# A Fourier layer stack with 3x3 convolutions in one kernel: halo kept once, side columns and corners as 32x32 products

## The chip, the cores and the metric

The kernel runs on one core of a Trainium2 chip. The metric is device time in microseconds (us), the median of several executions. Five engines work beside each other, each through its own instruction stream: PE (TensorE, matmuls), DVE (VectorE), ACT (ScalarE), POOL (GpSimd, which also issues the stores here) and SP (SyncE, which issues the loads). They meet at semaphores.

## The reference, cut to what matters

```python
h = concatenate([grid, x]) @ P_w + P_b                  # 32 images of 64x64, 32 channels
for i in range(4):
    h_ft = rfft2(h)
    out_modes = einsum('bixy,ioxy->boxy', h_ft[:, :, :16, :16], w_c)   # w_c complex
    spec = irfft2(out_modes, s=(64, 64))
    conv = conv_general_dilated(h, conv_w[i], (1, 1), 'SAME') + conv_b[i]   # 3x3
    h = leaky(spec + conv)
out = leaky(h @ Q1_w + Q1_b) @ Q2_w + Q2_b              # the "head", one value a pixel
h = out + attention(layernorm(out)); h = h + experts(layernorm(h))          # the tail
```

All of it is in fp32.

## The kernel before

Images go in pairs: 16 pairs a layer, 4 layers; `T = 16 * layer + pair` counts them. A pixel's parity in y and x (the "phase") stands on the partitions beside the 32 channels: 4 phases x 32 channels = 128 partitions, and a pair has 2 x 32 rows of 32 columns, cut in four units of 16 rows, one PSUM bank each (`acc[0]` to `acc[3]`, 512 columns).

One pair in the two middle layers (1 and 2, function `pair`) does this on PE. `convolve_centre` (L648): four products of 128x128 by 512 columns, one a unit, all taps that stay inside the 2x2 phase cell. `spectral` (L694): 64 products of 64x64 by 64 columns, the last step of the inverse transform, into the same four banks. `convolve_rows` (L662), twice: the taps that reach the phase cell above or below, and the corner taps. `rows_forward` (L553): the first transform of the pair's successor. `convolve_columns` (L676), twice: the taps to the left and right. `columns_back` (L620) and `columns_forward` (L566): two more transform steps of the next pair.

A product whose operands cover 64 partitions in and 32 out takes one of 8 places in the array, and 8 such products can run together; I call eight that fill the array (or one 128x128 product) a round of 512 columns. `convolve_rows` is 2 rounds a call, `convolve_columns` 1, so the edge work of a pair is 6 rounds in 48 products. The head's first product (`head_hidden`, L712) is of 32x32 by 512 columns. There are 16 a pair, in two groups of 8, since `hidden` has two banks.

The input of the convolution is `halo`, one pair's activations with a border, in SBUF in two copies: one with the phases ordered for rows, one for columns. They come from DRAM (`activations`), where POOL put them (`store`, four DMAs a pair) when the layer before made them: ACT evicts the four banks (`evict`, L1092) to `x_now`, DVE turns `x_now` (`turn_x`, L1283) into `xt` for `rows_forward`, `turn_rows` (L1289) and `turn_back` (L1312) turn the transform's other steps, ACT puts the spectrum away (`spectrum`, L346). SP loads the halo (`load_halo`, L406 and L412) when the pair two before has been accumulated.

Layer 0 convolves otherwise (L633), since its input is small. Between layers stands `boundary`: it needs the whole spectrum before `mix` (L605). In the last layer (`last_pair`) there is no forward transform; there PE also does the head of the pair before and steps of the tail, `fronts` (L735 to L769), put in by the table `SLOTS` at places 0, 1 and 2 of a pair. The order on each engine is the order of the code; waits are written out by hand.

Of the kernel before, what the change touches and what calls it, by code (L numbers as in the profile page):

```python
# [14 lines left out]
C = 32  # L15
NL = 4
MODES = 16
G = 32
# [4 lines left out]
HALO = TOP + PLANE + 2 * PITCH + 1  # L23
# [8 lines left out]
XCOL = 48  # L32

# [7 lines left out]
def dft_constants():  # L41
# [8 lines left out]
    for at in range(2):  # L50
        a = th * np.outer(2 * g + (at ^ (g >= 16)), k)
        ex[:, at, :, 0] = np.cos(a)
        ex[:, at, :, 1] = -np.sin(a)
# [8 lines left out]
    for qh in range(2):  # L62
        for kbh in range(2):
            for cg in range(2):
                for ql in range(2):
                    k1 = 4 * (2 * kbh + cg) + 2 * qh + ql
                    for il in range(2):
                        for at in range(2):
                            a = th * k1 * (4 * i16 + 2 * il + (at ^ (i16 >= 8)))
# [19 lines left out]
def build(nc, ser_d, xcol_d, fixed_d, dft_d, fold_w_d, fold_p_d, proj_d, spec_d, conv_d, convb_d,  # L89
# [4 lines left out]
    with ExitStack() as ctx:  # L94
# [16 lines left out]
        conv = sb("conv", [128, NL - 1, 512])  # L111
        centre = [conv[:, l, 0:256].rearrange("p (a n) -> p a n", a=2) for l in range(NL - 1)]
        edge_y = [conv[:, l, 256:320].rearrange("p (a n) -> p a n", a=2) for l in range(NL - 1)]
        edge_x = [conv[:, l, 320:448].rearrange("p (v a n) -> p v a n", v=2, a=2) for l in range(NL - 1)]
        corner = [conv[:, l, 448:512].rearrange("p (a n) -> p a n", a=2) for l in range(NL - 1)]
# [7 lines left out]
        halo = sb("halo", [128, 2, 2, HALO])  # L123
# [13 lines left out]
        hidden = psum[:, 4:6, :]  # L137
# [25 lines left out]
        s_side = [sem("s_side0"), sem("s_side1")]  # L163
# [64 lines left out]
        spare_h = flat(halo, "p k a n -> p (k a n)")  # L228
        squares = spare_h[:, 0:1024].rearrange("p (k n) -> p k n", k=2)
        spread = spare_h[:, 1024:2048].rearrange("p (k n) -> p k n", k=2)  # L230
        late = spare_h[:, 2048:8192].rearrange("p (a k n) -> p a k n", a=6, k=2)
        alive = spare_h[:, 2048:4096].rearrange("p (b s) -> p b s", b=B)
        fx, live, hx, hm, ht, fo = (late[:, n] for n in range(6))
# [96 lines left out]
        def units(T):  # L330

            return (0, 1, 2, 3) if T < PAIRS else (0, 2, 1, 3)

        def evicted(T, u):

            return 4 * T + units(T).index(u) + 1
# [36 lines left out]
        def halo_loads(T):  # L373

            return 128 * ((T - PAIRS) // 2 + 1)
# [3 lines left out]
        def _(sp):  # L379
# [15 lines left out]
            def load_halo(T):  # L395
                l, p = place(T)
                k, src = T % 2, T - PAIRS
                sp.wait_ge(s_store[src % 2], 64 * (src // 2 + 1))
                if src >= 2:
                    sp.wait_ge(s_acc, 4 * (T - 2) + 4)  # L400
                n = 2 * UNIT
                for h in range(2):
                    to, of = TOP + n * h, n * h
                    for f in range(4):
                        g = 32 * (2 * (f % 2) + (f // 2 ^ h))
                        sp.dma_start(halo[32 * f:32 * f + 32, k, 0, to:to + n],  # L406
                                     x_d[p, g:g + 32, of:of + n]).then_inc(s_halo[k], 16)
                for h in range(2):
# [1350 lines left out]
```

## Time and profile before

| | |
|---|---|
| median of 3 runs | 1119.27 us (1118.8 to 1122.3) |
| profiled execution, its own time | 1122.64 us |
| its span | 1120.5 us |
| PE busy | 1049.3 us (94%) |
| DVE, ACT, POOL busy | 604.0, 464.3, 152.9 us |
| granted PE clock, mean | 0.985 |
| moved by DMA | 194.27 MB |

The span is what the trace covers; the execution's own time has about 2 us more around it. Busy shares are means over four layers and a tail of different kinds. "issue" in a row is time in which an engine waited for nothing that the profile shows. A product in fp32 stands in the trace as two weight loads and two matmuls, so `x64` in a row of L662 is 32 products.

### The profile page before, as it was taken

The numbers are of one execution on the slowest core, as the hardware profiler recorded it, in microseconds if no ns is written. First come the engines' busy times: TensorE is split into PE (matmuls) and PEld (weight loads), VectorE is DVE, ScalarE is ACT, GpSimd is POOL, SyncE is SP. The second block draws the span as 40 slices with busy tenths as digits, with TensorE's granted clock in tenths as the row PEclk, the third lists the DMA queues.
The fourth block names the chain that finished last, engine by engine and source line by source line (L and its number), as shares of the span: only waits on it lengthen the run. The fifth ranks groups of instructions, "written<-read, shape, count | busy, mean of one in ns | idle before, by whom it ended". The sixth has DMA issues, their size and how long they took to land.

```text
span 1120.5 us, 48730 instructions
## 1 busy us (share of the span) xinstructions
PE 1049.3 (94%) x22512; PEld 556.8 (50%) x22512; DVE 604.0 (54%) x560; ACT 464.3 (41%) x895; POOL 152.9 (14%) x299
## 2 busy tenths in 40 slices
PE   5899998899999999899999998999999999899985
PEld 2555554555555554654555555434444334366743
DVE  5688788655556665555556565201322303387844
ACT  3356553323333333133343342232443534666524
POOL 2022221011111111011111110102112121300000
PEclk9999998999999999999999999999999999899998
DMA  9277768279888888488988886578766453000001
GB/s 321 60 221 214 200 176 249 84 216 270 252 260 258 254 232 238 137 245 254 258 257 267 234 237 192 148 163 197 188 144 147 120 125 82 8 2 1 1 1 19
DMA packets 66714, 194.27 MB, mean 173 GB/s; under 512 B 22256, under 2 KB 24816, under 8 KB 59248
## 3 DMA queue, kind: packets, MB, share of 16 engines
q1 hardware_dynamic: 54224, 138.19, 45.4%
q0 software_dynamic: 12288, 52.97, 16.5%
q8 instruction: 177, 2.90, 1.1%
q14 instruction: 25, 0.20, 0.1%
HBM read 138.13 MB, written 52.95 MB: 171 GB/s over the span
## 4 chain that ended last, share of the span: by engine, by line
PE 84%; DVE 7%; issue 5%; ACT 3%; DMA 0%; DVEq 0%; ACTq 0%
PE psum L662 16%; PE psum L648 15%; PE psum L694 11%; PE psum L676 7%; PE psum L620 5%; PE psum L566 4%; PE psum L553 4%; PE psum L633 4%; PE psum L712 3%; PE psum L605 2%; PE psum L903 2%; PE psum L720 1%; DVE xt L1283 1%; DVE ft L1289 1%; DVE vt L1312 1%
## 5 line engine op out<-in xcount | busy, mean ns | idle before, releaser
L1092 ACT ACTIVATE x_now<-psum,conv_bias 128x512 f32<-128x512 f32 x256 | 155.2, 691 | 321.6 <-PE psum L676 248.4
L1312 DVE STREAM_TRANSPOSE vt<-psum 128x1024 f32<-128x1024 f32 x64 | 126.2, 1972 | 198.8 <-PE psum L620 198.8
L1283 DVE STREAM_TRANSPOSE xt<-x_now 128x1024 f32<-128x1024 f32 x100 | 199.4, 2032 | 15.1 <-ACT x_now L1092 8.9
L1289 DVE STREAM_TRANSPOSE ft<-psum 128x1024 f32<-128x1024 f32 x50 | 100.5, 2010 | 188.4 <-PE psum L553 188.4
L662 PE MATMUL psum<-halo,conv 64*32 64x512 f32 x3072 | 189.0, 593 | 3.5 <-issue 3.4
L346 ACT ACTIVATE spec<-psum 32x128 f32<-32x128 f32 x372 | 143.7, 386 | 92.3 <-PE psum L566 88.5
L648 PE MATMUL psum<-halo,conv 128*128 128x512 f32 x384 | 178.0, 605 | 0.7 <-ACT x_now L1092 0.7
L497 POOL DMA_DIRECT2D activations<-x_now x192 | 94.3, 492 | 600.4 <-PE psum L662 408.5
L694 PEld LDWEIGHTS psum<-dft,vt 64*64 64x64 f32 x8192 | 126.5, 135 | 50.0 <-issue 49.8
L694 PE MATMUL psum<-dft,vt 64*64 64x64 f32 x8192 | 135.8, 220 | 2.2 <-issue 2.2
L648 PEld LDWEIGHTS psum<-halo,conv 128*128 128x128 f32 x384 | 68.5, 188 | 83.5 <-issue 74.7
L662 PEld LDWEIGHTS psum<-halo,conv 64*32 64x32 f32 x3072 | 55.1, 106 | 107.0 <-issue 104.8
L676 PE MATMUL psum<-halo,conv 64*32 64x512 f32 x1536 | 97.0, 591 | 0.0
L620 PE MATMUL psum<-zt,dft 64*32 64x256 f32 x2048 | 77.5, 377 | 10.1 <-issue 7.1
L553 PE MATMUL psum<-xt,dft 64*32 64x512 f32 x800 | 62.1, 602 | 13.5 <-DVE xt L1283 11.1
L620 PEld LDWEIGHTS psum<-zt,dft 64*32 64x32 f32 x2048 | 46.4, 106 | 52.3 <-issue 41.8
L1099 ACT ACTIVATE xt<-psum,q1b 128x512 f32<-128x512 f32 x64 | 40.5, 683 | 68.5 <-PE psum L712 68.3
L566 PEld LDWEIGHTS psum<-dft,ft 128*32 128x32 f32 x3200 | 48.5, 111 | 37.6 <-DVE ft L1289 28.9
L633 PE MATMUL psum<-xcol,conv 96*128 96x512 f32 x128 | 64.7, 632 | 0.4 <-ACT x_now L1092 0.4
L566 PE MATMUL psum<-dft,ft 128*32 128x64 f32 x3200 | 57.5, 223 | 7.2 <-DVE ft L1289 4.5
L504 POOL DMA_DIRECT2D tower_out<-ft x64 | 31.8, 504 | 206.1 <-ACT ft L1106 190.0
L676 PEld LDWEIGHTS psum<-halo,conv 64*32 64x32 f32 x1536 | 31.0, 106 | 50.6 <-issue 45.5
(158 smaller groups left out, 800.5 us busy)
## 6 DMA issues: line engine op xcount, KB each, us to landing
halo<-activations SPq DMA_DIRECT2D x768, 132.0 KB, 3.4
activations<-x_now POOLq DMA_DIRECT2D x192, 264.0 KB, 4.3
wspec<-in_spec SPq DMA_DIRECT2D x64, 256.0 KB, 5.4
xcol<-in_xcol SPq DMA_DIRECT2D x16, 384.0 KB, 5.4
x_now<-in_ser SPq DMA_DIRECT2D x2, 1024.0 KB, 6.5
spec<-in_onehot SPq DMA_DIRECT2D x8, 256.0 KB, 5.7
wspec<-in_causal SPq DMA_DIRECT2D x8, 256.0 KB, 6.2
consts<-in_tail SPq DMA_DIRECT2D x6, 185.0 KB, 5.7
```

What stands on the lines that cost most here:

```text
L346: return copy(spec[g:g + 32, 64 * qh:64 * qh + 64, ql, 2 * p:2 * p + 2].rearrange("p (y x) b -> p y b x", x=MODES), columned(X + 2)[32 * q ...
L566: z = mm(columned(n)[g:g + 32, 64 * kyb:64 * kyb + 64], ft[:, k0, :], ey[:, ri, :], start=(ri == 0), stop=(ri == 1))
L620: z = mm(backed[g:g + 32, cg, 256 * ri:256 * ri + 256], iy[64 * cg:64 * cg + 64, m, 32 * h:32 * h + 32], zt[64 * cg:64 * cg + 64, :, 2 * p ...
L633: mm(acc[u], conv0[:, u // 2, :], xcol[0:96, k, HALF * u:HALF * u + HALF], start=True, stop=False, skip_group_check=True)
L648: mm(acc[u], centre[l - 1][:, u // 2, :], window(T, 0, None, u, 0, 0), start=True, stop=False, skip_group_check=True)
L662: z = mm(acc[u][g:g + 32, :], weight[64 * f:64 * f + 64, s, :], window(T, 0, f, u, di, dj), start=False, stop=False, skip_group_check=True)
L676: z = mm(acc[u][g:g + 32, :], edge_x[l - 1][64 * f:64 * f + 64, h, r, :], window(T, 1, f, u, 0, -1 if s == 0 else 1), start=False, stop=p > 0,
L694: z = mm(acc[u][64 * s:64 * s + 64, at:at + 64], vt[64 * il:64 * il + 64, k, 4 * u + ih].rearrange("p r o -> p (r o)"), ix[64 * il:64 * il ...
L1092: copy(x_now[:, k, 16 * u:16 * u + 16, 0:G], acc[u].rearrange("p (i j) -> p i j", j=G), ACT.Prelu, bias=conv_bias[:, l:l + 1], alpha=SLOPE ...
L1283: vec.transpose(xt[:, 32 * m:32 * m + 32, :], src).then_inc(s_xt, 1)
L1289: vec.transpose(ft[:].rearrange("p k c -> p c k"), rowed.rearrange("p a b -> p (a b)").rearrange("p (i c) -> p c i", c=C)).then_inc(s_ft, 1)
L1312: vec.transpose(vt[:, k].rearrange("p h r o -> p (h r) o").rearrange("p y o -> p o y"), backed.rearrange("p a b -> p (a b)").rearrange("p ...
```

## The change

The halo is kept once (rows order only), with three things for it.

- Phases of a unit are stored in another permutation, one that depends on the unit's half and parity (`u // 2`, `u % 2`). `load_halo` becomes one DMA of 128 partitions and four of 32 (was 16 of 32). `store` becomes eight DMAs (was four), each with half the rows, and they wait for other points of PE's work.
- The edge work of a pair is 5 rounds in 64 products: `convolve_rows`, 2 calls of 8 products of 64x32, one round each, without the corners; `convolve_sides`, 3 calls of 16 products of 32x32, for corners (tap 0), and side columns (taps 1 and 2). Tap 2 runs ahead of `rows_forward`, taps 0 and 1 at the pair's end, after `columns_back`. All four banks are complete only with tap 1.
- `hidden` has four banks (4 to 7) and `head_hidden` is one group of 16 products. The `fronts` of places 0 and 1 come behind it, each behind a wait for ACT to have read two of these banks.

```diff
-                n = 2 * UNIT
-                for h in range(2):
...
-                        sp.dma_start(halo[32 * f:32 * f + 32, k, 0, to:to + n],
-                                     x_d[p, g:g + 32, of:of + n]).then_inc(s_halo[k], 16)
...
+                sp.dma_start(halo[:, k, TOP:TOP + REACH], x_d[p, :, 0:REACH]).then_inc(s_halo[k], 16)
+                for f in range(4):
+                    g = 32 * (f ^ 1)
+                    sp.dma_start(halo[32 * f:32 * f + 32, k, TOP + REACH:TOP + 2 * REACH],
+                                 x_d[p, g:g + 32, PLANE - REACH:PLANE]).then_inc(s_halo[k], 16)
...
-                    elif i == 2:
-                        pool.wait_ge(s_fx, P + 2)
-                    elif i == 3:
-                        pool.wait_ge(s_acc, 4 * P + 2)
                     else:
-                        pool.wait_ge(s_seg, 2 * (P - PAIRS) + 1 + i)
...
+                    elif i < 2:
+                        pool.wait_ge(s_half, 2 * P + 1 + i)
+                    else:
+                        pool.wait_ge((s_fx, s_v)[i - 2], P + 2)
+                    rows = x_now[32 * i:32 * i + 32, X % 2].rearrange("p (h w i) j -> p w h (i j)", h=2, w=2)
+                    for w in range(2):
+                        g = 32 * (2 * (i % 2 ^ w) + i // 2)
+                        pool.dma_start(x_d[X % PAIRS, g:g + 32].rearrange("p (h w n) -> p w h n", h=2, w=2)[:, w],
+                                       rows[:, w]).then_inc(s_store[X % 2], 16)
...
+            def convolve_rows(T, h):
+                for s in range(2):
+                    for f in range(2):
+                        for w in range(2):
+                            r, u = 1 - f, 2 * h + w
+                            g, part = 32 * (2 * s + (r ^ w)), slice(64 * f, 64 * f + 64)
+                            mm(acc[u][g:g + 32, :], edge_y[l - 1][part, h, s, :],
+                               window(T, part, u, (-1 if r == 0 else 1), 0), start=False, stop=False,
...
+            def convolve_sides(T, tap):
+                if tap == 0:
+                    pe.wait_ge(s_seg, T - PAIRS + 1)
+                for u in range(4):
+                    h, w = u // 2, u % 2
+                    for a in range(2):
+                        for b in range(2):
+                            r, s = (a if tap == 2 else 1 - a), 1 - b
+                            g, f = 32 * (2 * s + (r ^ w)), 32 * (2 * a + (b ^ h))
+                            part = slice(f, f + 32)
+                            z = mm(acc[u][g:g + 32, :], sides[l - 1][part, tap, h, :],
+                                   window(T, part, u, 0 if tap > 0 else -1 if r == 0 else 1, -1 if s == 0 else 1),
+                                   start=False, stop=(tap == 1 and p > 0), skip_group_check=True)
+                    if tap == 1 and p > 0:
+                        z.then_inc(s_acc, 1)
+                if tap == 2:
+                    z.then_inc(s_seg, 1)
...
+            def head_hidden(p):
+                pe.wait_ge(s_x, 4 * ((NL - 1) * PAIRS + p) + 4)
+                reached(pe, s_h, p)
+                for u in range(4):
                     for g in range(4):
-                        to = 32 * (g ^ (u % 2))
+                        to = 32 * (g ^ u)
...
             def last_pair(p):
...
+                    convolve_sides(T, 2)
+                    fronts_read(p - 1, 2)
+                    head_hidden(p - 1)
+                    convolve_rows(T, 0)
+                    pe.wait_ge(s_hid, 4 * (p - 1) + 2)
                     fronts(p, 0)
-                    fronts_read(p - 1, 2)
-                    head_hidden(p - 1, 0)
-                    convolve_rows(T, 0)
                     convolve_rows(T, 1)
+                    pe.wait_ge(s_hid, 4 * (p - 1) + 4)
                     fronts(p, 1)
-                    head_hidden(p - 1, 2)
-                    convolve_columns(T, 0)
-                    convolve_columns(T, 1)
+                    convolve_sides(T, 0)
+                    convolve_sides(T, 1)
```

On PE, one pair of a middle layer before, in products: L648 is the centre, L694 the inverse transform, L662 the rows and corners, L553 the forward rows, L676 the columns, L620 and L566 the other transform steps.

```order
L648 MATMUL psum<-halo,conv 128x512 x4
L694 MATMUL psum<-dft,vt 64x64 x64
L662 MATMUL psum<-halo,conv 32x512 x32
L553 MATMUL psum<-xt,dft 32x512 x8
L676 MATMUL psum<-halo,conv 32x512 x16
L620 MATMUL psum<-zt,dft 32x256 x16
L566 MATMUL psum<-dft,ft 32x64 x32
```

The same pair now; the lines have moved: L637 is the centre, L684 the inverse transform, L664 `convolve_sides`, L543 the forward rows, L648 `convolve_rows`, L610 and L556 the other transform steps.

```order
L637 MATMUL psum<-halo,conv 128x512 x4
L684 MATMUL psum<-dft,vt 64x64 x64
L664 MATMUL psum<-halo,conv 32x512 x16
L543 MATMUL psum<-xt,dft 32x512 x8
L648 MATMUL psum<-halo,conv 32x512 x16
L610 MATMUL psum<-zt,dft 32x256 x16
L664 MATMUL psum<-halo,conv 32x512 x32
L556 MATMUL psum<-dft,ft 32x64 x32
```

`rows_forward` stands behind 16 edge products instead of 32, and the last 32 are of the 32x32 kind, between two other kinds.

On PE, the pair of the last layer that carries steps S (L744) and E (L749) of the tail, before: L712 is the head's first product, L720 its second.

```order
L648 MATMUL psum<-halo,conv 128x512 x4
L694 MATMUL psum<-dft,vt 64x64 x64
L744 MATMUL psum<-proj 64x64 x8
L712 MATMUL psum<-x_now,q1w 32x512 x8
L662 MATMUL psum<-halo,conv 32x512 x32
L749 MATMUL psum<-consts,series 128x128 x4
L712 MATMUL psum<-x_now,q1w 32x512 x8
L676 MATMUL psum<-halo,conv 32x512 x16
L620 MATMUL psum<-zt,dft 32x256 x16
L720 MATMUL psum<-xt,q2w 32x512 x4
```

Now, with L699 the head's first product, L731 and L736 the steps S and E, L707 the head's second product:

```order
L637 MATMUL psum<-halo,conv 128x512 x4
L684 MATMUL psum<-dft,vt 64x64 x64
L664 MATMUL psum<-halo,conv 32x512 x16
L699 MATMUL psum<-x_now,q1w 32x512 x16
L648 MATMUL psum<-halo,conv 32x512 x8
L731 MATMUL psum<-proj 64x64 x8
L648 MATMUL psum<-halo,conv 32x512 x8
L736 MATMUL psum<-consts,series 128x128 x4
L664 MATMUL psum<-halo,conv 32x512 x32
L610 MATMUL psum<-zt,dft 32x256 x16
L707 MATMUL psum<-xt,q2w 32x512 x4
```

Between S and E there stand 8 products now, where there were 40; and S stands behind the head's 16.

On ACT at the same place before: L1099 evicts the head's hidden layer, L1122 is the exponential of step S, L1126 the copy of step E.

```order
L1106 ACTIVATE ft<-psum,q2b 128x512
L1122 ACT_TABLE_LOAD
L1122 ACTIVATE series<-fold_p 64x4x64 x2
L1099 ACTIVATE xt<-psum,q1b 128x512 x2
L1126 ACTIVATE fold_w<-psum 128x512
L1099 ACTIVATE xt<-psum,q1b 128x512 x2
L1092 ACTIVATE x_now<-psum,conv_bias 128x16x32 x4
```

And now, with L1089, L1112 and L1116 in their places:

```order
L1096 ACTIVATE ft<-psum,q2b 128x512
L1089 ACTIVATE xt<-psum,q1b 128x512 x4
L1112 ACT_TABLE_LOAD
L1112 ACTIVATE series<-fold_p 64x4x64 x2
L1116 ACTIVATE fold_w<-psum 128x512
L1082 ACTIVATE x_now<-psum,conv_bias 128x16x32 x4
```

The table load and the exponential now stand behind all four evictions of the hidden layer.

## Rows read from the trace of the kernel before

**Rows 1.** The page: busy time and instructions of each engine.

```profile
PE 1049.3 (94%) x22512; PEld 556.8 (50%) x22512; DVE 604.0 (54%) x560; ACT 464.3 (41%) x895; POOL 152.9 (14%) x299
```

**Rows 2.** Chain of waits, one middle-layer pair: start us, us, what.

```profile
584.79 3.64 PE psum L648 x8
588.43 2.02 PE psum L694 x128
590.45 3.60 PE psum L662 x64
594.05 0.86 PE psum L553 x16
594.91 1.72 PE psum L676 x32
596.63 0.86 PE psum L620 x32
597.49 1.03 PE psum L566 x64
```

**Rows 3.** The same view, one last-layer pair without a tail step.

```profile
762.05 1.02 PE psum L712 x16
763.07 3.60 PE psum L662 x64
...
767.68 1.88 PE psum L676 x32
769.56 0.86 PE psum L620 x31
770.42 0.99 PE psum L720 x8
```

**Rows 4.** Stretches, layers 1 and 3: us, each engine's busy us, clock, DMA share, GB/s.

```profile
231.76:442.33 210.57, 209.88 (x5134) 110.33 (x5129) 122.96 (x66) 80.64 (x175) 29.38 (x60) 1.00 0.88 252
709.43:947.07 237.64, 236.14 (x4418) 96.98 (x4419) 54.38 (x83) 98.58 (x161) 39.47 (x78) 1.00 0.63 152
```

**Rows 5.** Chain of waits: a stall inside L662.

```profile
620.11 0.89 issue
```

**Rows 6.** Timeline of PE, eight starts: start, us from first start to last end.

```profile
898.33 0.66 PE L712 MATMUL psum<-x_now,q1w 32*32 32x512 f32 x8
```

**Rows 7.** Groups by line: busy us, mean ns of one, idle before.

```profile
L712 PE MATMUL psum<-x_now,q1w 32*32 32x512 f32 x512 | 34.8, 600 | 0.9 <-DVE sq L1340 0.9
```

**Rows 8.** Timeline of ACT, then DVE, behind one pair's last round.

```profile
639.07 2.42 ACT L1092 ACTIVATE x_now<-psum,conv_bias 128x512 f32<-128x512 f32 x4 [8.01 <-PE psum L676]
641.83 3.21 ACT L346 ACTIVATE spec<-psum 32x128 f32<-32x128 f32 x8 [0.34 <-PE psum L566]
...
642.79 4.09 DVE L1283 STREAM_TRANSPOSE xt<-x_now 128x1024 f32<-128x1024 f32 x2
```

**Rows 9.** Timeline of ACT, last layer: table load, step S, hidden evictions.

```profile
873.79 1.28 ACT L1122 ACT_TABLE_LOAD   x1
881.09 0.84 ACT L1122 ACTIVATE series<-fold_p 64x256 f32<-64x256 f32 x2 [6.02 <-DVE fold_p L1362]
...
899.53 1.26 ACT L1099 ACTIVATE xt<-psum,q1b 128x512 f32<-128x512 f32 x2 [3.25 <-PE psum L712]
```

**Rows 10.** Chain of waits: step S on PE.

```profile
879.67 0.46 PE psum L744 x16
```

**Rows 11.** Chain of waits at the boundary into layer 3, some of its pieces.

```profile
680.46 2.41 ACT x_now L1092 x4
...
700.97 1.88 PE psum L662 x32
702.85 0.95 PE psum L620 x32
...
708.71 0.68 ACT x_now L1092
```

**Rows 12.** The page, DMA issues: KB each, median us to landing.

```profile
activations<-x_now POOLq DMA_DIRECT2D x192, 264.0 KB, 4.3
```

More of the change, by code:

```diff
@@ L110, in build @@
         conv_bias = sb("conv_bias", [128, NL])
[L111 to L115, printed above, removed]
+        conv = sb("conv", [128, NL - 1, TAPS])
+        centre = [conv[:, l, 0:512].rearrange("p (h w n) -> p h w n", h=2, w=2) for l in range(NL - 1)]
+        edge_y = [conv[:, l, 512:640].rearrange("p (h s n) -> p h s n", h=2, s=2) for l in range(NL - 1)]
+        sides = [conv[:, l, 640:832].rearrange("p (t h n) -> p t h n", t=3, h=2) for l in range(NL - 1)]
         fold_w = sb("fold_w", [128, 4, 128])
@@ L136, in build @@
         backed = psum[:, 6:8, :]
-        hidden = psum[:, 4:6, :]
+        hidden = psum[:, 4:8, :]
         valued = psum[:, 4, :]
@@ L810, in pair @@
                     return
-                for u in units(T):
+                for u in range(4):
                     convolve_centre(T, u)
@@ L827, in last_pair @@
                 if p > 0:
-                    for u in units(T):
+                    for u in range(4):
                         convolve_centre(T, u)
@@ L853, in boundary @@
                 T = l * PAIRS
-                for i, u in enumerate(units(T - 1)):
+                for u in range(4):
                     convolve_centre(T, u)
-                    if l == 1 and i == 1:
+                    if l == 1 and u == 1:
                         columns_forward(T)
+                convolve_sides(T, 2)
                 rows_forward(T + 1)
@@ L1647, in phases @@
         q = a.reshape(n, G, 2, G, 2).transpose(4, 2, 0, 1, 3)
[L1648 removed]
+        return np.concatenate([q[:, ::1 - 2 * (u % 2), :, 8 * u:8 * u + 8] for u in range(4)], axis=3)
     ser = np.zeros((2, 2, 2, C, G, 2, PITCH), np.float32)
@@ L1696, in tower_inputs @@
         for b in range(2):
-            for r in range(2):
+            for h in range(2):
                 for s in range(2):
-                    centre[a, b, :, :, 0, s, r] = tap(a - r, b - s)
-                    centre[a, b, :, :, 1, s, 1 - r] = tap(a - r, b - s)
-                edge_x[b, a, :, :, 0, r] = tap(a - r, 1 - 2 * b)
-                edge_x[1 - b, 1 - a, :, :, 1, r] = tap(a - r, 1 - 2 * b)
-            for s in range(2):
-                edge_y[a, b, :, :, s] = tap(1 - 2 * a, b - s)
-                if b != s:
-                    corner[a, b, :, :, s] = tap(1 - 2 * a, 2 * s - 1)
-    conv = np.concatenate([a.reshape(128, NL - 1, -1) for a in (centre, edge_y, edge_x, corner)], axis=2)
+                    for r in range(2):
+                        for w in range(2):
+                            centre[a, b ^ h, :, :, h, w, s, r ^ w] = tap(a - r, b - s)
+                    edge_y[a, b ^ h, :, :, h, s] = tap(1 - 2 * a, b - s)
+                out = 1 - 2 * b
+                sides[a, b ^ h, :, :, 0, h] = tap(1 - 2 * a, out)
+                sides[a, b ^ h, :, :, 1, h] = tap(2 * a - 1, out)
+                sides[a, b ^ h, :, :, 2, h] = tap(0, out)
+    conv = np.concatenate([a.reshape(128, NL - 1, -1) for a in (centre, edge_y, sides)], axis=2)
     fold_p = np.zeros((4, C, 4, 2, 48), np.float32)
```

144 lines of the change are left out of this document (49 added, 95 removed).

## The prediction

> **What bounds the kernel now.** I read the page's busy line first: PE is busy 94% of the span, DVE 54%, ACT 41% [rows 1]. Then the chain of waits through one pair of a middle layer: it stays on PE from end to end, in seven blocks that add up to 13.73 us [rows 2]. So a middle pair costs what PE's blocks cost, and what the others do beside it is hidden as long as none of it ends after PE arrives. The last layer's pair replaces L553 and L566 by two head blocks of 1.02 and the head's second product, 0.99, and its L676 costs 1.88 [rows 3]; with L648 and L694 as in rows 2 it is 15.03 us. The stretches tell what lies above that floor: layer 1 spends 210.57 us on 15 pairs, against 15 x 13.73 = 205.95, so 4.6 us of stalls, at a DMA share of 0.88 [rows 4]. One such stall is 0.89 us of "issue" inside L662 [rows 5].
>
> **The price of a round.** L553 and L676 are one and two rounds of the 64x32 kind behind the same kind: 0.86 and 1.72 [rows 2]. L662 is four, 3.44, and costs 3.60, since it follows L694, which is 64x64. L712, a round of eight 32x32 products, costs 1.02, and L676 behind it 1.88 in place of 1.72 [rows 3]. So a change of kind costs 0.16 us. Eight products start one after another: 0.66 us from the first start to the last end [rows 6], one alone 0.60 [rows 7], so starts are 7 to 8 ns apart. Sixteen reach 0.05 us further, and the next kind waits for the last of them.
>
> **Middle pairs (30, 15 in each of layers 1 and 2).** Removed: one of six edge rounds, -0.86. Added: two changes of kind (32x32 to 64x32 ahead of `rows_forward`, back behind `columns_back`; the others are in the rows already), +0.32, and twice the longer tail of sixteen, +0.10. Net -0.44 a pair, if sixteen 32x32 products fill a round as eight 64x32 do: -13.2 us. That price is the one thing no row of before shows. Its lower end is 0.86, what 512 columns cost in every kind of these rows that fills or half fills the array. Its upper end is that only eight of this kind run at once, as L712's do [rows 3]: 1.72. I take 0.86: issue is not near a limit, since L694 gets through 64 products in 2.02 us, 32 ns each [rows 2], where sixteen in 0.86 need 54 ns.
>
> The Trainium skill speaks against this in TensorEngine Tiling (Array Packing), "Gotcha 1: PSUM Pressure": different row tiles cannot access the same PSUM bank at once. Here the four products of a unit are of four row groups and go to one bank. The trace has this already and does not agree: L712's eight products are four row groups into each of two banks, and they cost 1.02 with the change of kind [rows 3].
>
> In TensorE: Matmul & The Clock Gate, "Part 3: Packing small matmuls — row/col tiling", the Trainium skill has sixteen 32x32 products together at 10.6 times one, and a reorder window of 64 entries on PE. By that page a round of sixteen, each product two loads and two matmuls (L712 has 512 matmuls for 256 products [rows 7]), just fits. No row here shows it.
>
> **Do the waits stay hidden?** All four banks now end together, in tap 1. From the start of L712 at 898.33 [rows 6] to ACT's start behind it at 899.53 [rows 9] there are 1.20 us. So if R is the start of the last round, ACT starts to evict at R+1.16 (the first bank needs four of the sixteen). Four evictions take 2.42, one 0.69 of it [rows 8]: the first bank is free at R+1.85, all at R+3.6. PE does `columns_forward` from R+1.05 to R+2.15, so the centre product does not wait (0.3 to spare). DVE's two turns, 4.09 [rows 8], end at R+7.75. PE comes to `rows_forward` after 1.05 + 1.10 + 3.64 + 2.02 + 1.07: R+8.9, 1.1 to spare. ACT's spectrum, 3.21 [rows 8], ends at R+6.8, and is needed at the same point. All hidden; if the turn came later than that, each tenth would cost 3 us over 30 pairs. POOL's eight store issues lie beside 13 us of PE (POOL is busy 14% [rows 1]). SP issues 5 loads for 16, and the halo bytes fall from 16 x 32 x 4224 B = 2.16 MB to 2 x 128 x 4488 B = 1.15 MB a pair.
>
> **Last layer (15 pairs).** New blocks: 3.64 + 2.02; then one stretch of 32x32 with a sides round and the head round, 1.72 + 0.16 + 0.05 = 1.93; rows, 1.88; two sides rounds, 1.93; then 0.86 and 0.99: 13.25, against 15.03. But PE now waits for ACT. With H the start of the head round, ACT starts at H+1.24 (1.20 and the longer tail). Two evictions take 1.26 [rows 9], the second two end 1.14 later. The wait for two ends at H+2.56, where PE arrives at H+1.93: 0.63 lost. The wait for four ends at H+3.69, where PE arrives at H+3.58: 0.11, and 0.03 of restart. So 14.02, -1.0 a pair. In the three pairs with steps S and E it is less: ACT is at the hidden evictions until H+3.64, then loads its table, 1.28, then does the exponentials, 0.84 [rows 9]; in the old order the load ran in an earlier gap. E can start at H+5.82; S, 0.46 [rows 10] and a change of kind, and a round have taken PE to H+4.15: 1.67 lost, so -0.3 in these three. Sum: 12 x 1.0 + 3 x 0.3 = -12.9 us.
>
> **Boundaries (3).** The rows call behind `mix` is one round instead of two and lies on the chain: 1.88 [rows 11] becomes 1.02, -2.6 in three. The evictions ahead of it, 2.41 [rows 11], start 0.8 later against the end of the rounds than when two banks were ready early: +1.6 for the two boundaries that follow such a pair. The sides rounds lie beside `turn_back`. The store two pairs back now waits for `columns_back`, which ends at 703.80; two issues and 4.3 us to landing [rows 12] end about 709, where the eviction that needs it stands at 708.71 [rows 11]: +0.4 twice. Sum -0.2. The end of the last pair, one head round earlier but waiting for ACT either way: -0.5, from -1 to 0.
>
> **Stalls.** Layer 1 has 4.6 us above its floor [rows 4]. Fewer bytes should shorten such stalls, 64 products for 48 lengthen them: 0, from -6 to +5 in all. Layer 0 keeps its PE work: 0, from -2 to +3 for the doubled store issues.
>
> **The sum.** -13.2 - 12.9 - 0.2 - 0.5 = -26.8. The profiled execution took 1122.6 us by its own time (1120.5 its span), so 1095.8. It stands 3.4 above the median shown, 1119.3, and I forecast on the median: 1092.5.
>
> **Rivals.**
> 1. *Eight at once.* Of the 32x32 kind only eight products run together, and a round of sixteen costs 1.72. There are 48 convolutions with three such rounds, 144, and 16 head rounds: 160 x 0.86 = +138, so 1230. For it: the rows show eight together, never sixteen. Against: the sixteen have sixteen places of their own, and the eight of L712 run at full rate in half of them. From 26.8 / 160 = 0.17 us a round on, the kernel is slower than before.
> 2. *A short window.* All sixteen run together, but behind each change of kind the second eight start 0.28 us late, because PE's queue does not reach so far: two such blocks in 48 convolutions, 96 x 0.28 = +27, so 1119, no change. At a third of that 1101. Nothing in the rows reaches past eight, so nothing speaks against it but that L694's issue is quick.
> 3. *The turn is late.* DVE and ACT end 2 us later than rows 8 give: L553 waits 0.9 in 30 pairs, +27, 1119. Against: four blocks of PE stand between.
> 4. *Stalls grow* by half a us in 45 pairs, since more instructions have to be brought in behind L694: +22, 1115. Against: DMA has less to move.
> 5. *Row groups take turns at a bank.* The four row groups of a unit run one after another, 3.44 a round, +2.58 x 160 = +413, so 1505. Against: L712 [rows 3]. The bank rule of the Trainium skill's page above is this.
>
> **Chances.** The forecast, with its own range 1083 to 1102: 0.66. Rivals 2, 3 or 4 in part (1102 to 1115.9): 0.15. In full, within 0.3% of before (1115.9 to 1122.6, which a measurement cannot tell from no change): 0.05. Slower: rival 1, 0.09; rival 5, 0.01; a stronger rival 2, 0.04. So faster by over 0.3% 0.81, within 0.05, slower 0.14. The range that leaves out two tenths is 1082 to 1113.
>
> **What would show it.** A middle pair at 13.3, with its two sides blocks at 1.07 and 1.93; under rival 1 they are 1.9 and 3.6, under rival 2 the pair is 13.7 to 13.9 and the block behind the inverse transform near 1.3. Rival 3 shows `rows_forward` waiting for DVE. In the last layer: PE waiting for the hidden evictions, 0.6 and 0.1 us a pair, pairs of 14.0, and in three pairs for the exponential. DMA share in layer 1 falls from 0.88 to about 0.7. I am wrong if sixteen 32x32 products behind their own kind cost over 1.0 us.

## The result, and the profile after

The changed kernel takes 1143.05 us (median of 4 runs, 1138.25 to 1144.38) against 1119.03 for the kernel before in the same comparison: recorded ratio 1.0185, 95% interval 1.015 to 1.0219 (the two medians alone give 1.0215). It is slower, by about 2%; the forecast was 1092.5, with a range from 1082 to 1113. The profiled execution took 1141.75 us, its span 1139.6. By stage of the two profiled spans (us); a pair's period runs from its first centre product to the next pair's, the last pair's to the next layer's:

| | before | after | |
|---|---|---|---|
| layer 1, 15 pair periods; shortest | 210.57; 13.73 | 211.23; 13.69 | +0.7 |
| layer 2, 15; shortest | 212.14; 13.73 | 218.38; 13.69 | +6.2 |
| layer 3, 14; shortest | 237.64; 15.03 | 242.99; 14.81 | +5.3 |
| from the last pair's centre products to the end | 173.4 | 179.3 | +5.9 |
| all else, boundaries among it | 286.8 | 287.7 | +0.9 |

The page's lines for PE, for the group of the 32x32 products, and for the queue that brings instructions (packets, MB, share of 16 engines):

```profile
PE 1049.1 (92%) x24048; PEld 554.5 (49%) x24048; DVE 609.0 (53%) x560; ACT 459.4 (40%) x895; POOL 261.6 (23%) x491
L664 PE MATMUL psum<-halo,conv 32*32 32x512 f32 x4608 | 177.0, 607 | 5.4 <-issue 5.1
q8 instruction: 189, 3.10, 1.2%
```

PE is busy as long as in [rows 1], in a longer span: rounds were removed and their time was not gained. POOL's busy time grew from 152.9 to 261.6 with twice the store issues, and nothing on the chain waits for it.

The chain of waits through a middle pair without a stall (start us, us, what), which answers to [rows 2]. L637 is `convolve_centre`, L684 `spectral`, L664 `convolve_sides`, L543 `rows_forward`, L648 `convolve_rows`, L610 `columns_back`, L556 `columns_forward`:

```profile
580.55 3.64 PE psum L637 x8
584.19 2.02 PE psum L684 x128
586.22 1.09 PE psum L664 x32
587.31 1.05 PE psum L543 x16
588.36 1.72 PE psum L648 x32
590.08 0.86 PE psum L610 x32
590.94 2.28 PE psum L664 x62
593.22 1.03 PE psum L556 x64
```

The sum is 13.69. One round of sixteen behind another kind is 1.09, near the forecast (1.07); two together are 2.28 where 1.93 was forecast. The timeline of PE's weight loads inside that 2.28 (start us, first start to last end, count) shows where it goes:

```profile
590.87 0.25 PEld L664 LDWEIGHTS psum<-halo,conv 32*32 32x32 f32 x32 [0.41 <-issue]
591.33 0.10 PEld L664 LDWEIGHTS psum<-halo,conv 32*32 32x32 f32 x1 [0.20 <-issue]
591.76 0.10 PEld L664 LDWEIGHTS psum<-halo,conv 32*32 32x32 f32 x1 [0.33 <-issue]
591.95 0.37 PEld L664 LDWEIGHTS psum<-halo,conv 32*32 32x32 f32 x30
```

A product in fp32 is two loads and two matmul passes. The 32 loads of the first sixteen products go out within 0.25 us. The two loads of the seventeenth follow at 591.33 and 591.76, each as soon as the weights that it replaces are in use. The next load comes only at 591.95, though the eighteenth's place had come as far as the seventeenth's 0.01 us behind it. The first product's second pass ran from 591.33 for 587 ns, so 591.95 is 0.03 us behind its end (starts are recorded, ends of matmuls are the profiler's model). From there loads come in wider steps (30 in 0.37 us): 16 to 17 ns from product to product, against about 7 in the first ten of a round.

The stretches of layers 1, 2 and 3, which answer to [rows 4] (us, busy of each engine, clock, DMA share, GB/s):

```profile
232.69:443.92 211.23, 208.93 (x5608) 106.54 (x5609) 125.43 (x66) 78.13 (x173) 66.20 (x124) 1.00 0.73 183
471.42:689.80 218.38, 212.35 (x5608) 107.86 (x5608) 125.27 (x66) 78.19 (x173) 67.04 (x126) 0.99 0.71 177
717.33:960.32 242.99, 228.56 (x4866) 96.46 (x4866) 54.80 (x83) 97.04 (x160) 42.47 (x83) 0.99 0.37 94
```

The DMA share fell, in layer 1 as forecast (0.88 to 0.73) and in layer 3 too (0.63 to 0.37), and it bought nothing: above 15 x 13.69 there are 5.9 us in layer 1 and 13.0 in layer 2, where before had 4.6 and 6.2 above 15 x 13.73. Nearly all of it is stalls; in layer 2 some 1.7 us are the lower clock, which was granted for 3.4 us behind the longest of them. The longest of them, in the chain (answering to [rows 5]), and the instruction queue in the stretch 478.2 to 479.4:

```profile
477.14 1.08 PE psum L664 x30
478.22 2.48 issue
480.70 1.45 PE psum L664 x2
```

```profile
q8 instruction: 1, 0.02, 5.7%
```

PE stops behind fifteen of sixteen products, and the profile shows no semaphore that holds it. One packet of instructions (3.10 MB in 189, so 16.4 KB each) is under way from 478.27 to 479.36, and PE goes on 1.34 us later. The long "issue" stalls that I followed in the two traces end 1.3 to 1.6 us behind such a packet; one of 0.47 us, in layer 3 of the kernel before, ends 1.73 behind.

In the last layer the chain through a pair without a tail step, answering to [rows 3] (L699 is the head's first product, L707 its second):

```profile
756.41 1.09 PE psum L664 x32
757.50 1.20 PE psum L699 x32
...
759.31 1.85 ACT xt L1089 x3
...
761.20 2.35 PE psum L664 x62
763.54 1.02 PE psum L610 x32
764.57 0.97 PE psum L707 x5
```

PE's rows products are no longer on it: it goes through ACT's four evictions of the hidden layer. The pair takes 14.81, where 14.02 was forecast. In a pair with steps S and E:

```profile
824.77 1.28 ACT L1112
...
826.06 0.42 ACT series L1112
...
826.49 0.42 ACT series L1112
...
827.05 0.63 PE psum L736 x4
```

The table load and both exponentials lie on the chain, as the prediction had them.

### The profile page after: what moved, and what is told of

It is laid out like the page before. It is cut to its first block, busy times and chain, and to the rows that moved or that the text cites. A ratio compares the mean times of both kernels' runs of the same rounds, so it can differ in the third digit from the quotient of the medians.

```text
span 1139.6 us, 51379 instructions
## 1 busy us (share of the span) xinstructions
PE 1049.1 (92%) x24048; PEld 554.5 (49%) x24048; DVE 609.0 (53%) x560; ACT 459.4 (40%) x895; POOL 261.6 (23%) x491
## 4 chain that ended last, share of the span: by engine, by line
PE 48%; ACT 5%; DVE 3%; issue 3%; ACTq 0%; DVEq 0%
PE psum L664 10%; PE psum L637 10%; PE psum L684 6%; PE psum L610 3%; PE psum L648 2%; ACT xt L1089 2%; PE psum L699 2%; PE psum L894 2%; PE psum L543 2%; PE psum L556 1%; PE psum L595 1%; PE psum L707 1%; PE psum L747 1%; PE psum L911 1%; PE psum L944 1%
## 5 line engine op out<-in xcount | busy, mean ns | idle before, releaser
L487 POOL DMA_DIRECT2D activations<-x_now x384 | 203.3, 556 | 502.3 <-PE psum L684 218.9
L664 PE MATMUL psum<-halo,conv 32*32 32x512 f32 x4608 | 177.0, 607 | 5.4 <-issue 5.1
L637 PE MATMUL psum<-halo,conv 128*128 128x512 f32 x384 | 178.0, 605 | 1.0 <-ACT x_now L1082 1.0
L684 PEld LDWEIGHTS psum<-dft,vt 64*64 64x64 f32 x8192 | 127.1, 135 | 55.0 <-issue 54.9
L684 PE MATMUL psum<-dft,vt 64*64 64x64 f32 x8192 | 137.2, 220 | 6.5 <-issue 6.4
L637 PEld LDWEIGHTS psum<-halo,conv 128*128 128x128 f32 x384 | 68.8, 189 | 83.6 <-issue 61.8
L648 PE MATMUL psum<-halo,conv 64*32 64x512 f32 x1536 | 103.9, 596 | 4.5 <-ACT xt L1089 2.8
L664 PEld LDWEIGHTS psum<-halo,conv 32*32 32x32 f32 x4608 | 53.1, 103 | 69.1 <-issue 57.0
L610 PE MATMUL psum<-zt,dft 64*32 64x256 f32 x2048 | 78.3, 378 | 8.1 <-issue 5.8
L1089 ACT ACTIVATE xt<-psum,q1b 128x512 f32<-128x512 f32 x64 | 38.9, 688 | 103.2 <-PE psum L699 103.2
L543 PE MATMUL psum<-xt,dft 64*32 64x512 f32 x800 | 60.6, 619 | 14.5 <-DVE xt L1272 10.7
L556 PEld LDWEIGHTS psum<-dft,ft 128*32 128x32 f32 x3200 | 49.3, 113 | 47.4 <-issue 30.5
L610 PEld LDWEIGHTS psum<-zt,dft 64*32 64x32 f32 x2048 | 44.1, 106 | 55.1 <-issue 41.6
L556 PE MATMUL psum<-dft,ft 128*32 128x64 f32 x3200 | 57.6, 226 | 6.0 <-DVE ft L1278 5.9
L648 PEld LDWEIGHTS psum<-halo,conv 64*32 64x32 f32 x1536 | 29.6, 106 | 62.1 <-issue 51.3
```

The source lines that it names most:

```text
L487: pool.dma_start(x_d[X % PAIRS, g:g + 32].rearrange("p (h w n) -> p w h n", h=2, w=2)[:, w], rows[:, w]).then_inc(s_store[X % 2], 16)
L556: z = mm(columned(n)[g:g + 32, 64 * kyb:64 * kyb + 64], ft[:, k0, :], ey[:, ri, :], start=(ri == 0), stop=(ri == 1))
L610: z = mm(backed[g:g + 32, cg, 256 * ri:256 * ri + 256], iy[64 * cg:64 * cg + 64, m, 32 * h:32 * h + 32], zt[64 * cg:64 * cg + 64, :, 2 * p ...
L637: mm(acc[u], centre[l - 1][:, u // 2, u % 2, :], window(T, slice(0, 128), u, 0, 0), start=True, stop=False, skip_group_check=True)
L648: mm(acc[u][g:g + 32, :], edge_y[l - 1][part, h, s, :], window(T, part, u, (-1 if r == 0 else 1), 0), start=False, stop=False, skip_group_ ...
L664: z = mm(acc[u][g:g + 32, :], sides[l - 1][part, tap, h, :], window(T, part, u, 0 if tap > 0 else -1 if r == 0 else 1, -1 if s == 0 else 1 ...
```

## The experiments

Each total is a median, and each ratio is to the kernel before, which ran beside them at 1117.9 to 1118.8. Stages and pairs are read from one profiled execution of each.

**One half of the change at a time.** The new convolution with the head of before:

```diff
-                    head_hidden(p - 1)
+                    head_hidden(p - 1, 0)
                     convolve_rows(T, 0)
...
+                    head_hidden(p - 1, 2)
```

> The changed convolution (halo once, 5 edge rounds) with the old head: two groups of 8 products, tail steps where they stood. Theory A (the new convolution gains nothing because sixteen products run into a short window on PE, and the loss of the changed kernel comes mostly from the head's placement: waits for ACT in the last layer, late exponential, lower clock in the tail): 1120 to 1128 us; last-layer pairs without a tail step near 14.8 us; no PE wait for the hidden evictions; the clock stays full between 960 and 1000 us. Rival B (the convolution's order itself costs the 24 us, by stalls and the window, and the head is neutral): 1138 to 1145.

Measured: 1129.46 (1127.01 to 1132.87), ratio 1.0104 (1.004 to 1.0169). This is nearest to theory A, 1.5 above its range: the shortest last-layer pair is 14.90, and the clock stays full from 960 to 1000. Layer 2 is 219.07, as long as with the whole change, layer 3 is 236.60.

The convolution of before with the head in one group of sixteen:

> The old convolution with the new head: one group of 16 products and the tail steps behind it. Theory A: the head alone costs 8 to 14 us (waits of 0.7 us in 15 pairs, less 0.8 us of one round saved, 1.7 to 2 us more in each of three pairs with the exponential, some 6 us by a lower clock behind the last pair): 1127 to 1133. Rival B: within 3 us of before, 1116 to 1122.

Measured: 1118.15 (1114.22 to 1124.28), ratio 0.9995 (0.9967 to 1.0024). The shortest last-layer pair is 14.34 against 15.03, yet its 14 periods sum to 240.35 against 237.64. The grouping saved 14 x 0.69, 9.7 us; stalls named issue took 10.4 us there against 1.5, and the clock was low for 6.8 us (3.4 lost) where before it was never low. Rival B held and theory A fell: no pair shows the waits that it named. So the convolution alone costs some 11 us, the head alone nothing, and the two together 24.

**The order in the last layer.** The changed kernel with its front products moved: those of place 0 stand behind both rows calls, those of place 1 and the wait for all four evictions behind the last two sides rounds, and all of them use one bank:

```diff
                     convolve_rows(T, 0)
+                    convolve_rows(T, 1)
                     pe.wait_ge(s_hid, 4 * (p - 1) + 2)
                     fronts(p, 0)
-                    convolve_rows(T, 1)
-                    pe.wait_ge(s_hid, 4 * (p - 1) + 4)
-                    fronts(p, 1)
                     convolve_sides(T, 0)
                     convolve_sides(T, 1)
+                    fronts(p, 1)
+                    pe.wait_ge(s_hid, 4 * (p - 1) + 4)
```

> The changed kernel with one thing moved: in the last layer both rows calls stand directly behind the head's sixteen products, the tail's steps of place 0 behind them (bank 5, so only two evictions are waited for) and those of place 1 behind the sides rounds. Theory A: the waits of PE for the hidden evictions go (0.77 us in 12 pairs), the exponential is covered in three pairs (about 2 us each), and if the clock in the tail fell because of these waits it stays up: 1120 to 1130. Rival C (the waits are only moved: DVE, ACT and the evictions get late instead): over 1138.

Measured: 1120.39 (1116.52 to 1130.36), ratio 1.0018 (0.9983 to 1.0053), 22.7 less than the changed kernel. Theory A held, rival C fell. Its stretch of layer 3, and PE's timeline in a pair without a tail step:

```profile
716.77:944.21 227.44, 223.61 (x4866) 97.95 (x4866) 54.71 (x83) 95.54 (x160) 42.48 (x83) 1.00 0.40 100
```

```profile
754.19 1.41 PE L699 MATMUL psum<-x_now,q1w 32*32 32x512 f32 x32
755.52 2.13 PE L648 MATMUL psum<-halo,conv 64*32 64x512 f32 x32
757.58 2.35 PE L664 MATMUL psum<-halo,conv 32*32 32x512 f32 x64
```

The rows products are one block again, with no wait in it; the pair is 14.29 and the layer 15.6 shorter. Another 7.6 are in the end (171.6 against 179.3), where the clock stands low for less time; other kernels with the same order don't keep that (below).

The same order with the convolution of before:

> The convolution of before, the head's first product in one group, and the front products and the centre of the next pair issued ahead of the wait for the hidden evictions. Theory A (in the last layer TensorE waits about 0.8 us a pair for the hidden evictions only because little work stands between the grouped product and its reader; the gain of that order, 14.81 to 14.29 us for the shortest pair with the new convolution, is there with the old one too): shortest last-layer pair 13.8 to 14.3 us against 15.03 before, total 1107 to 1114. Rival B (that order helped the new convolution only, by how its code lies against the instruction fetches): shortest pair stays at 14.3 to 15.0, total 1116 to 1122.

Measured: 1119.76 (1116.42 to 1127.14), ratio 1.002 (0.9995 to 1.0046). Theory A fell: the shortest pair is 14.34 with either order of the grouped head. There the 3.70 us of L662 stand behind the grouped product and cover ACT's evictions; the new convolution has 1.9 in their place, and so gains from the other order.

**Rows products ahead of the first sides round**, in middle pairs, to move the stalls:

```diff
+                convolve_rows(T, 0)
+                convolve_rows(T, 1)
                 convolve_sides(T, 2)
                 rows_forward(T + 1)
-                convolve_rows(T, 0)
-                convolve_rows(T, 1)
```

> The changed kernel with one thing moved in the middle layers: both rows calls ahead of the tap 2 sides round and of the forward rows, so that PE uses up its instructions more slowly behind the 64 small products. Theory D (the long stalls named issue, 0.9 to 2.5 us, are instruction fetches that begin when PE has too little left to do): stalls in layers 1 and 2 fall by about half, total 1134 to 1139. Rival E (the stalls stand at fixed places of the stream or come from DMA traffic): within 2 us of the changed kernel, 1141 to 1145.

Measured: 1143.49 (1136.64 to 1147.81), ratio 1.0214. The shortest pair is 13.86, a change of kind more; the stalls stayed (7.1 and 11.2 us above the floor in layers 1 and 2). Theory D fell and rival E's range holds: this reordering behind the 64 small products does not remove them.

**The size of a round.**

```diff
+                half = l == 1 and tap < 2 and p > 0
-                for u in range(4):
+                for u in range(2 if half else 4):
...
                 convolve_sides(T, 0)
+                if l == 2:
+                    convolve_sides(T, 1, True)
                 convolve_sides(T, 1)
```

> The changed kernel, with the size of the side and corner rounds altered in two layers: layer 1 issues only 8 of the 16 products in each of the first two rounds (the side and corner taps of units 2 and 3 of these two are left out of the result), layer 2 issues the second round twice (that tap is counted twice). Theory A (16 products of a round hold all places on TensorE until they complete, so that the next 16 begin late and in wider steps): in layer 1 the two rounds of 8 together take 1.85 to 1.95 us less the missing products' starts, so 1.75 to 1.95 against 2.28 and a shortest pair of 13.2 to 13.4; in layer 2 the third contiguous round costs 1.05 to 1.20, shortest pair 14.75 to 14.9. Rival B (a 32x32 product, or the change to it, is dear by itself, however many are in flight): layer 1's block stays at 2.15 or more, and layer 2's extra round costs 0.86, shortest pair 14.55.

Measured, one run: 1153.88. The side products (L665 here) in the chain, two rounds of eight in layer 1 and three of sixteen in layer 2:

```profile
260.75 1.88 PE psum L665 x32
...
592.18 3.33 PE psum L665 x91
```

Theory A holds by all its numbers. Two rounds of eight cost 1.88, which is 0.86 + 1.02 as the price from [rows 3] has it, with nothing lost, and the shortest pair is 13.29. A third round of sixteen costs 1.05 to 1.06 (3.34 less 2.28), the shortest pair is 14.75.

**Where the code lies.** The queue q8 tells how many of PE's instructions come in a packet: the kernel before had 177 packets for 45,024 loads and matmuls of PE, the changed one 189 for 48,096, so 12 more packets for 3,072 more instructions, 256 in each. With the instructions that only wait or signal, a middle pair had 694 in the trace, so each began 74 places earlier in its block of 256 than the pair before; now it has 756 and moves by 12. Places are counted in PE's compiled stream; counted from the first record of a trace of the new convolution they are 5 lower. In the changed kernel's layer 2 the 64 small products (`spectral`) of pairs 1 to 6 begin at places 138 to 78; these are the long pairs (18.79, 15.25, 16.63, 15.12, 14.24, 15.13). To test it, everything behind the first boundary was moved:

```diff
                 convolve_sides(T, 2)
+                idle_products(T - 1, {1: 32}.get(l, 0))
```

> The changed kernel with 32 idle products put into the wait between layers 0 and 1, where TensorE stands still anyway: all later code lies 128 instructions further on, and nothing else is altered. Theory G (which pairs lose time is set by where a boundary of 256 instructions falls in them; it costs when it falls within the 64 small products of the spectral part): the excess over the shortest pair moves. In layer 1 it grows from 5.7 us to 10 to 18 us, in layer 2 the first six pairs, now 12.9 us over, come down to under 5 us in all, and the seventh to thirteenth, now under 1 us, rise to 6 to 14 us. Rival H (the stalls belong to the place in the program, as the first pairs after a layer's start): the same pairs stay long, each within 1 us of what it was. Total 1136 to 1150 by G, 1141 to 1144 by H.

Measured, one run: 1144.7. The stretches of layers 1 and 2:

```profile
232.42:455.86 223.44, 213.79 (x5608) 106.50 (x5608) 125.15 (x66) 78.00 (x173) 66.01 (x124) 1.00 0.69 173
485.34:699.53 214.19, 210.06 (x5614) 106.67 (x5608) 125.42 (x66) 77.64 (x173) 67.01 (x126) 1.00 0.72 181
```

The stalls moved with the code. Layer 1's excess over its shortest pair went from 5.9 to 18.1: the ten pairs at places 186 down to 78 take 14.31 to 16.94, the next three (66 to 42) 13.70. In layer 2 the long pairs are now those at 182 to 110; six of the first seven take 13.70. H fell. (The first pair behind the boundary, at place 198, took 15.39; that pair is long in layer 1 of every kernel with the new convolution, 15.08 or more.)

Then the pair was made 768 instructions long, three blocks of 256, on top of the late order in the last layer:

```diff
+                idle_products(T, 3)
                 convolve_sides(T, 2)
...
+                idle_products(T - 1, {1: 42}.get(l, 0))
```

> The new convolution with the late order of the last layer (the kernel that took 1120.39 us), and idle products added so that a middle pair has 768 instructions on TensorE, three times 256: 3 a pair (some 0.05 us each pair), and 42 in the wait between layers 0 and 1, so that the boundary of 256 falls at the same place of every middle pair, outside the 64 small products. Theory G: nearly all middle pairs take 13.70 to 13.80 us, the excess of layers 1 and 2 (together some 18 us) falls to under 4, total 1103 to 1110. Rival H (stalls come from the fetches' number or from other traffic, wherever the boundary falls): total 1118 to 1124, the excess stays above 12 us.

Measured: 1111.51 (1104.69 to 1114.23, 10 runs), ratio 0.9932 (0.9904 to 0.996). The excess of the two layers fell to 3.1 us, as G has it; the total is 1.5 above G's range. And with the same pairs, only at other places:

```diff
-                idle_products(T - 1, {1: 42}.get(l, 0))
+                idle_products(T - 1, {1: 78, 2: 49}.get(l, 0))
```

> The kernel with 3 idle products in every middle pair (1111.51 us, all its middle pairs 13.8 us but for five), with the filling between the layers changed so that the boundary of 256 instructions falls in the middle of the 64 small products of every pair of layer 1 (their first instruction stands at place 126 of its 256), and in layer 2 near their end (place 58). The pairs themselves hold the same instructions. Theory G (the place of the boundary decides): layer 1's middle pairs take 14.5 to 16.5 us each, 10 to 30 us more than at place 238; layer 2's stay at 13.8 to 14.0, as pairs at places 30 to 66 did before; total 1123 to 1145. Rival (the three idle products themselves, or an even number of instructions, brought the gain): both layers stay at 13.8, total 1110 to 1116.

Measured: 1165.5 (1157.17 to 1171.63), ratio 1.0418 (1.0373 to 1.0463). The stretches of layers 1 and 2, first at places 238 and 230, then at 126 and 58:

```profile
234.43:442.98 208.55, 207.67 (x5700) 110.16 (x5699) 125.60 (x66) 77.68 (x172) 64.98 (x122) 1.00 0.74 184
472.64:681.18 208.54, 207.91 (x5703) 110.08 (x5699) 125.55 (x66) 77.70 (x172) 67.03 (x126) 1.00 0.74 186
```

```profile
232.93:486.17 253.24, 230.74 (x5699) 107.33 (x5699) 124.64 (x66) 78.07 (x173) 66.12 (x124) 0.96 0.61 153
515.95:728.31 212.36, 209.97 (x5699) 109.31 (x5699) 124.97 (x66) 78.05 (x173) 66.97 (x126) 1.00 0.73 182
```

The same 15 periods of the same instructions take 208.55 or 253.24. In the second kernel every one of layer 1 stalls, behind the same instruction; the chain in one (L846 are the idle products):

```profile
308.45 2.02 PE psum L684 x128
310.48 0.11 PE psum L846 x6
310.59 1.06 PE psum L664 x30
311.65 1.65 issue
313.30 1.30 PE psum L664 x2
```

G's direction holds and its size was too small (44.7 more, where 10 to 30 was expected): the stalls are 0.5 to 2.6 us each, and the clock was low for 20 us in this layer, so some 10 of the 44.7 are the clock's. Layer 2 at 58 is only 5 us above its floor, so neither the idle products nor the count's being a multiple of 256 decides, but the place.

The last kernel takes smaller idle products and puts the 42 where PE waits longest:

```diff
-                    mm(psum[64 * s:64 * s + 64, 6 + il, ...
+                    mm(psum[32 * s:32 * s + 32, 6, c:c + 8], ...
...
                 columns_forward(T + 1)
+                idle_products(T - 1, {1: 42}.get(l, 0))
                 mix(l)
```

> The aligned kernel again (place 238), with idle products of 32x32 and 8 columns in place of 64x64 and 64 columns, and the 42 between the layers moved from a place where TensorE waits 0.4 us to one where it waits 1.9. Theory (the filling costs its own time only): 13.72 to 13.78 us a middle pair against 13.81, and 1 to 2 us less in the first boundary: 1105 to 1110 in all. Rival (a change of tile form costs as much as it saves): 13.80 to 13.90 a pair, total 1110 to 1114.

Measured: 1109.71 (1106.67 to 1119.9, 12 runs), ratio 0.9936 (0.9909 to 0.9963). The pair did not get shorter (13.82): the idle products cost 0.11 in either size. The first boundary did, 29.93 for 32.08. So the theory was wrong on the pair and right on the boundary. This kernel and the aligned one can't be told apart; both are 0.6 to 0.7% faster than the kernel before, by intervals that leave out 1, and faster than the changed one.

## Why the prediction was wrong

The sum said -26.8 against the profiled 1122.6; the profiled execution after stands at +19.1. The 45.9 between them, by the terms of the sum (the stages not named below make up the last 1.1):

**Middle pairs, -13.2: mis-sized; 12.0 of the miss.** The pair saves 0.04 in place of 0.44. The part that failed is "sixteen 32x32 products fill a round as eight 64x32 do". For the first round they do (1.09); a round right behind another costs 1.19, and a third 1.06. I named this as rival 2, a short window, but looked for it behind a change of kind, where it isn't: the loss is at the second sixteen. Rounds of eight don't have it. What fits all of this, and is not shown, is that sixteen products, four instructions each, fill the 64 places that the Trainium skill gives PE's reorder window (TensorE: Matmul & The Clock Gate, "Part 3: Packing small matmuls — row/col tiling"), and that a place comes free only when a product is complete. I had read "just fits" as no loss. The run shows that it fits once; the loads above agree with a wait for completion, the number 64 itself only the page gives, and no run separates a limit on loads from one on matmuls. My sign of being wrong, over 1.0 us for such a round behind its kind, was the right one.

**Stalls, 0 (from -6 to +5): wrong in kind; 8.1 of the miss in layers 1 and 2.** I asked what the DMAs do and how many products there are. Neither decides: the DMA share fell and the stalls grew; two kernels with the same pairs differ by 44.7 us in one layer. It is the place of the small products in PE's stream of instructions. The edit changed it throughout, from steps of 74 places a pair, with one pair in three or four long, to steps of 12, which keep bad ones in a row: six in layer 2 here, ten in the shifted kernel. Rival 4 had the sign, a price (+22) and half the cause: instructions have to be brought in, but where a block ends decides, not how many there are. The Trainium skill has the blocks of 256 instructions (Runtime: NRT & Kernel Launch, "Instruction fetch mechanics") and calls their crossing mostly hidden. The packets of this trace agree on the size; on the hiding the runs decide otherwise, 0.5 to over 4 us a pair at bad places, with the clock behind it.

**Last layer, -12.9 (-12.6 in the 14 periods of the table, which grew by 5.3): some 18 of the miss.** ACT is as forecast: the last of its four evictions lets PE go on at H+3.70 (757.50 to 761.20), where I had 3.69, and table load and exponentials lie on the chain in full. What stands around them failed in three terms. The sides round ahead of H is 1.09, where the sum left 0.86 for it. The two rounds behind are 2.35, not 1.93. L610 behind them is a change of kind, 1.02, which I had priced at 0.86. Together 0.81 by the rows, 0.79 by the pairs (14.81 less 14.02), 9.5 us in the 12 pairs without steps S and E.

For the pairs with S and E my -0.3 does not follow from my own terms: with E at H+5.82 they add up to 3.64 + 2.02 + 0.86 + 5.85 + 0.59 + 1.93 + 0.86 + 0.99 = 16.7, against 16.1 for such a pair before, so +0.7. By the chain, without stalls and the step of place 2, it is 17.6, +1.5: for the two such pairs of these periods 3.7 us of the miss. The rest is 3.3 us of stalls named issue (4.8 against 1.5) and 1.7 us by a stretch of 3.4 us at the lower clock, which before did not have there. I also took the order of the waits as given, where moving them alone takes 15.6 us off these periods.

**The end, -0.5: 5.9 more instead; with the -0.3 of the third pair with S and E, which lies here, 6.7 of the miss.** No step of mine spoke of the clock. Stretches that hold the lower level, 1.2 GHz of 2.4, first two after, then one before (same columns as above):

```profile
972.00:975.00 3.00, 1.92 (x27) 1.03 (x37) 0.86 (x2) 1.52 (x4) 0.00 (x0) 0.62 0.00 0
...
986.40:1000.00 13.60, 12.13 (x44) 6.25 (x40) 5.27 (x8) 7.45 (x12) 6.99 (x13) 0.50 0.07 12
```

```profile
970.00:978.00 8.00, 6.51 (x22) 3.10 (x14) 2.63 (x5) 4.28 (x6) 4.39 (x9) 0.59 0.05 9
```

The clock was low for 3.4 us in the last pair and for 13.7 us later, 17.1 in all, against 6.8: half the difference, 5.1, is about the loss. The 0.8 left lie within what that third pair adds (1.5 in the other two). Ahead of the long stretch PE waits for ACT in the head's last pair: starts of its products are up to 1.25, 2.61 and 1.58 us apart there, where before had 1.17, 2.01 and 1.40.

The end follows the time at the lower clock in every kernel (us low, us of the end; the last 9 to 13 us, low in all of them, left out):

| kernel | low | end |
|---|---|---|
| new convolution, old head | 0 | 171.4 |
| late order; old convolution with late order | 3.4; 3.4 | 171.6; 171.2 |
| before; old convolution with grouped head | 6.8; 6.8 | 173.4; 173.2 |
| aligned with small idle products; shifted | 6.8; 6.8 | 172.7; 174.8 |
| aligned | 10.2 | 174.4 |
| at place 126; rows products first; round sizes | 13.7 each | 177.6; 178.2; 178.1 |
| changed | 17.1 | 179.3 |

The order of the last layer does not fix that time: four kernels with the late order and the new convolution have 3.4, 6.8, 10.2 and 13.7, the shifted kernel with the changed order 6.8. What brings the clock down there stays open.

**What held.** The four banks' later eviction stays hidden, as do the turn, the spectrum and POOL's issues; rivals 1, 3 and 5 are out (a round of sixteen is 1.09; `rows_forward` waits for nobody in the middle pairs; one bank takes four row groups at full rate). The three boundaries sum to 84.97 against 85.11, -0.1 where -0.2 was forecast. The DMA share of layer 1 is where it was forecast to be.

Open is what starts the fetch of a block: a bad place is known by experiment (about 75 to 190 for the start of the small products in this kernel), not derived. In the kernel before the range is another: in layer 1, with places counted from the trace's first record, the pairs at 179 and 185 take the shortest time, those at 105, 111, 139 and 145 are 0.7 to 1.1 us over. The last layer's pairs and layer 0 were not aligned.

## What to carry to other kernels

Price a round of small products by what a second one right behind it costs: here sixteen in flight held up the next sixteen, eight didn't. When a change alters the number of PE's instructions in a loop body, count them modulo 256 before and after; with quick products in the body a few idle ones that keep the place fixed can be worth more than the change itself (here 8.9 us for 0.11 a pair). When work is grouped, look at what is left between the producer and the wait for it. And when a stage near the end differs by a few us, look at the granted clock before explaining it by the code.

## What the runs showed of the hardware that was not expected

- Sixteen 32x32 products of 512 columns in fp32, each in its own place of the array: 1.09 us behind another kind, 2.28 for two rounds, 3.34 for three. Two rounds of eight: 1.88.
- The same 15 pair periods take 208.55 or 253.24 us by their place in the instruction stream alone.
- An idle product costs about 36 ns between busy ones (3 in 0.11 us), at 64x64 with 64 columns as at 32x32 with 8.
- Behind some stalls of 1.2 to 2.6 us the clock went to 1.2 GHz for 3.4 or 6.8 us (behind the one of 2.48 in layer 2 of the changed kernel for 3.4). In the kernel at place 126 one pass of a round there stands 0.81 us behind the pass before, in place of 0.41 to 0.43, and a stretch of it reads (clock third from the end):

```profile
242.00:249.00 7.00, 6.55 (x50) 1.50 (x58) 1.98 (x1) 0.00 (x0) 1.90 (x4) 0.52 0.48 112
```
